# State-space layers: the transfers of the chunk states are issued from ScalarE's queue instead of SyncE's

## The reference

```
for i in range(4):
    z = layernorm_channels(h, ln_w[i], ln_b[i])
    dtA = (-exp(A_re_log) + 1j * A_im) * exp(log_dt)
    C = (C_re + 1j * C_im) * expm1(dtA) / A
    K = 2 * Re(sum_n C * exp(dtA * l))          # l = 0 .. L-1
    y = gelu(causal_convolution(z, K) + z * D_skip)
    out = W @ y + b
    h = out[:H] * sigmoid(out[H:]) + h
```

## Time and profile before

| | us |
|---|---|
| median of 3 runs | 1290.07 (1289.85 to 1290.78) |
| profiled execution, its own time | 1292.57 |
| its span | 1290.80 |
| PE busy | 1026.0 (79%) |
| DVE busy | 774.5 (60%) |
| ACT busy | 529.7 (41%) |
| POOL busy | 418.0 (32%) |
| states' matmuls (725) start in the four layers at | 115.37, 200.67, 286.68, 368.17 |

### The profile page before, as it was taken

One profiled execution on the slowest core, in us unless ns is written; L12 is line 12 of the kernel. 1 busy time (PEld: TensorE's weight loads), 2 busy tenths in 40 slices (PEclk: granted clock), 3 DMA queues, 4 the chain that ended last, 5 costly groups with the idle time before them and its releaser, 6 DMA issues.

```text
span 1290.8 us, 20116 instructions
## 1 busy us (share of the span) xinstructions
PE 1026.0 (79%) x7980; PEld 692.3 (54%) x7980; DVE 774.5 (60%) x1349; ACT 529.7 (41%) x1231; POOL 418.0 (32%) x488
## 2 busy tenths in 40 slices
PE   6895876858545189999999777769889789979887
PEld 3563654636423167878787652334456534546643
DVE  2574574654827534646464668969756557956644
ACT  4646555356123311222212060026686514767732
POOL 0724403324106500000000125439843434954420
PEclk9976967669666589999999988979899899979989
DMA  3307135063144374334631210000111210012101
GB/s 94 73 7 143 32 62 109 6 100 71 23 78 197 66 139 98 98 97 75 120 68 29 92 66 1 0 1 0 34 35 39 58 65 26 1 34 51 43 9 33
DMA packets 60479, 76.50 MB, mean 59 GB/s; under 512 B 37500, under 2 KB 41992, under 8 KB 58632
## 3 DMA queue, kind: packets, MB, share of 16 engines
q1 hardware_dynamic: 60396, 75.36, 25.8%
HBM read 52.87 MB, written 1.51 MB: 42 GB/s over the span
## 4 chain that ended last, share of the span: by engine, by line
PE 51%; DVE 16%; POOL 14%; ACT 5%; SPq 5%; DMA 4%; issue 4%; POOLq 0%; DVEq 0%
PE psum L1189 7%; PE psum L1191 6%; PE psum L1190 6%; POOL rest L1426 3%; POOL rest L1416 3%; POOL rest L1422 2%; PE psum L693 2%; PE psum L1670 2%; SPq L1012 2%; POOL rest L1452 2%; DVE main L506 2%; SPq L1018 2%; PE psum L1716 2%; PE psum L1663 2%; DMA rest<-share_d 2%
## 5 line engine op out<-in xcount | busy, mean ns | idle before, releaser
L406 POOL TENSOR_TENSOR kept<-kept 128x8 f32<-128x8 f32 x8 | 1.6, 202 | 401.5 <-DVE kept L383 401.5
L1375 ACT ACTIVATE rest<-psum,main 128x128 f32<-128x128 f32 x256 | 113.3, 482 | 11.6 <-POOL main L1437 8.9
L1036 ACT ACTIVATE x_high<-main 128x512 fp32r<-128x512 f32 x48 | 30.3, 633 | 199.4 <-DVE main L1110 199.4
L1189 PE MATMUL psum<-x_high,w_low 128*128 128x512 f32 x192 | 76.9, 400 | 20.1 <-DVE x_low L1115 20.1
L1452 POOL TENSOR_TENSOR rest<-rest,main 128x512 f32<-128x512 f32 x64 | 65.4, 1042 | 34.6 <-DVE main L1522 34.6
L1189 PE MATMUL psum<-hid_high,w_low 128*128 128x512 f32 x192 | 75.6, 394 | 0.7 <-DVE main L1134 0.7
L1190 PE MATMUL psum<-x_low,w_high 128*128 128x512 f32 x192 | 76.2, 397 | 0.0
L1191 PE MATMUL psum<-x_high,w_high 128*128 128x512 f32 x192 | 76.1, 396 | 0.0
L1190 PE MATMUL psum<-hid_low,w_high 128*128 128x512 f32 x192 | 74.8, 389 | 0.0
L1191 PE MATMUL psum<-hid_high,w_high 128*128 128x512 f32 x192 | 74.7, 389 | 0.0
L1110 DVE TENSOR_TENSOR main<-kept,rest 128x512 f32<-128x512 f32 x48 | 33.1, 690 | 68.1 <-PE psum L1191 43.8
(11 more groups left out here) (316 smaller groups left out, 2841.2 us busy)
## 6 DMA issues: line engine op xcount, KB each, us to landing
rest<-share_d SPq DMA_DIRECT2D x4, 3072.0 KB, 21.4
rest<-share_d SPq DMA_DIRECT2D x4, 2304.0 KB, 20.4
main<-main SPq DMA_DIRECT2D x32, 256.0 KB, 5.2
main<-k_pad SPq DMA_DIRECT2D x16, 512.0 KB, 7.5
rest<-main SPq DMA_DIRECT2D x32, 256.0 KB, 3.5
main<-w_dram SPq DMA_DIRECT2D x2, 3072.0 KB, 14.0
main<-rest SPq DMA_DIRECT2D x32, 128.0 KB, 4.4
rest<-tables_dram SPq DMA_DIRECT2D x2, 2048.0 KB, 8.7
```

The source lines that it names most:

```text
L1189: T.matmul(dst, w_small, x_large, start=first, stop=False)
L1375: last = A.activation(probs[:, p, 4 * r + m, :], bank[2 * p + r][:, m * P:(m + 1) * P], ACT.Exp, scale=row_scale[:, c, r, m:m + 1], bias=r ...
```

## The change

In SP's part of a layer the loop of eight transfers is taken out. In ACT's part the same eight, with the same waits on `s4_u` and the same increments of `s4_u_moved`, stand behind the near sines and ahead of the far sines. In the last layer, where there are no sines, they stand behind the copies of `K`. ACT's wait for `s4_u` ahead of the gelu is dropped, as the transfers have waited for the same value.

```
@@ s4_act_layer
             if more:
                 s4_act_sines_near(act, L + 1)
+            for ri, src in ((0, u_re), (1, u_im)):
+                act.wait_ge(sem("s4_u"), L * 2 + ri + 1)
+                for g in range(GROUPS):
+                    at = CHUNK + MODES * ri
+                    act.dma_start(zu[at:at + MODES, HG * g:HG * (g + 1), :], src[32 * g:32 * g + 32]).then_inc(sem("s4_u_moved"), 16)
+            if more:
                 s4_act_sines_far(act, L + 1)
                 s4_act_magnitudes(act, L + 1, LOW_BANKS)
             A.activation(warm[:, 3 * L + 2:3 * L + 3], warm[:, 0:1], ACT.Gelu_apprx_tanh)
-            act.wait_ge(sem("s4_u"), L * 2 + 2)
@@ s4_sp_layer
-            for ri, src in ((0, u_re), (1, u_im)):
-                sp.wait_ge(sem("s4_u"), L * 2 + ri + 1)
-                for g in range(GROUPS):
-                    at = CHUNK + MODES * ri
-                    sp.dma_start(zu[at:at + MODES, HG * g:HG * (g + 1), :], src[32 * g:32 * g + 32]).then_inc(sem("s4_u_moved"), 16)
```

## The result

The changed kernel runs in 1284.78 us (median of 20 runs), the one before in 1290.12 (20 runs). The ratio is 0.9967, with a 95% interval of 0.9954 to 0.9980: 4.3 us less, between 2.6 and 5.9 (this is how far the means of the runs lie apart; the medians differ by 5.3). In a later comparison of the same two it was 0.9953 (0.9937 to 0.9968). The forecast was 1280.8, 9.3 us less. The direction was right, the size twice what was measured.

A forecast was written before the change was run, and what follows sets the result against it. Bound: Toeplitz reads, then states, filling the DMAs without pause ahead of PE. Gains of 2.3, 2.3 to 2.4, 2.3 and 2.3 us in layers 0 to 3 sum to 9.3, from 1290.07 to 1280.8; range 1276.5 to 1291.

The forecast's parts named there:

- What bounds the kernel: Ahead of PE's line 725: Toeplitz reads, then states, fill the DMAs without pause; PE idles 62.4 us in four layers.
- The landing: States' arrival ahead of PE: both streams mixed at 296 GB/s, 92 more than one, gain 2.3 us a layer.
- The hand-over: Quarter microsecond where Toeplitz reads give way to states on SP's queue: 288 and 304 GB/s, taken as the mixed rate.
- The full overlap: Rival at the states' landing: Toeplitz data alone end it, 4.5 us sooner; 12.9 us in all, 1277.2; chance 0.20.
- one stream at a time: Rival in the DMA engines: large and small packets taken in turn, 0.8 us a layer, 3.3 in all, 1286.8; chance 0.22.
- the estimate of 3.6 us: Sum over four layers if two halves at once give 6% of 15 us, by the Trainium skill.
- Held up: Rival at ACT's issues: stuck behind SP's backlog, ACT free at 111.53 in layer 0; 6 us slower, 1296; chance 0.16.
- What ACT pays: Ahead of the far sines: four u_im issues at 0.64, 2.56 us; ACT delayed 5.3, hidden under its wait for PE.
- The powers and POOL's norm: Work on DVE and POOL moving with ACT: powers to about 119.1 under the gelu; norm has some 8 us slack.
- Behind it every step shifts alike: After the last gelu of each layer: later steps move by the same gain, 2.3 us in layer 3.

The follow-up runs named there:

- (3): Changed kernel with the eight state transfers left out in layers 1 to 3; 1277.64 us, ratio 0.9891 to the kernel before (four runs).
- (1): Changed kernel with its state transfers cut into runs of 256 bytes by reversed row order; 1285.90 us, ratio 0.9966 to the kernel before.
- 2: Kernel before, one queue, with the four u_re transfers ahead of the fourth Toeplitz read; 1286.99 us, ratio 0.9979.
- 6: Kernel before, one queue, with the fourth Toeplitz read behind all eight state transfers; 1291.65 us, ratio 1.0004.
- 7: Changed kernel with the eight state transfers issued by GpSimd instead of ACT; 1285.15 us, ratio 0.9970 to the kernel before.
- 9: Changed kernel with each Toeplitz read spread over 128 partitions instead of 64 in layers 1 to 3; 1281.81 us, one run.
- (8): The changed kernel once more, unaltered, as a measure for other runs; 1283.65 us, ratio 0.9953 to the kernel before.
- (10): Kernel before, one queue, with the state transfers' bytes spread over all 128 partitions in layers 1 to 3; 1283.33 us, one run.
- (4): Changed kernel with only u_re issued by ACT, u_im by SP behind the Toeplitz reads; 1289.13 us, ratio 0.9994 to the kernel before.
- (5): Changed kernel with the state transfers' bytes spread over all 128 partitions in layers 1 to 3; 1278.82 us, one run.

## Why the prediction was off

**What bounds the kernel: right, and half heeded.** That the queue never pauses, and that 3.15 MB fill the time to the landing, was read from the earlier trace rows and holds. (3) shows it by taking the states' 1.05 MB out.

**The landing: the term that was mis-sized.** The step is "I take 2.3, as it is the only rate measured with both kinds in flight". The hand-over's quarter microseconds at 288 and 304 were taken for the rate of two streams running side by side. The stretch with two queues moves 230 and 233: 26 to 29 more than 204, for 8.7 us (the states' packets in layer 0 run from 6.1 to 14.9 us) instead of 5.1, so 26 x 8.7 / 204 = 1.1 us. The starts moved by 1.2 to 1.7; the rest, up to 0.6 us, is not accounted for.

The hand-over's rate wasn't even a rate. Its quarter microsecond in layer 0, before:

```profile
DMA packets 127, 0.07 MB, mean 288 GB/s; under 512 B 116, under 2 KB 116, under 8 KB 127
q1 hardware_dynamic: 127, 0.07, 157.1%
```

The view counts a packet's bytes in full where it starts (by its size classes 11 packets of 4 KB and 116 of 256 bytes or less). These eleven are 45 of the 72 KB, and one takes about 1.035 x 16 / 50 = 0.33 us (an estimate from the earlier trace rows), longer than the window. The packets that start in the window take 157% of the engines' time in it. With each packet's bytes spread over its own time, the trace gives 211 GB/s here and 207 in layer 1, hardly more than one stream's 203; over six microseconds around the hand-over the view itself shows no more than 212:

```profile
106.00:112.00 6.00, 0.00 (x0) 0.00 (x0) 3.00 (x4) 4.34 (x4) 0.76 (x2) 0.50 1.23 212
```

So no row of before measured two streams at once, and the 92 GB/s that the term was made of weren't there. The prediction had another objection among the words on its rival ("it may be different engines on different streams") and gave it too little weight; this trace can't tell whether that is so.

**The full overlap was out of reach.** Its argument, less than half of the rate of 455 for each stream, holds for the states (340 when spread) and not for the Toeplitz rows (218 when spread). That both move the same alone, 203 and 202, was read as one cause for both, and it is two. The overlap's own ceiling was a little low besides: 4.5 us, where the Toeplitz data alone in (3) gave 5.1 to 5.6.

**The rival "one stream at a time" came nearest**, with 0.8 us a layer and 1286.8, but by luck: its mechanism in the form given, by turns between a large and a small packet, would have left the Toeplitz data 1/16 of the bytes, and they had half. The Trainium skill (DMA: Bandwidth & Descriptors, Issuing engines are not separate DMA queues) says that DMAs of several issuing engines interleave on the same 16 and that only issue time is saved. The trace agrees with the first (0.91 and 0.93 MB side by side in 8 us) and not wholly with the second: the pair moves 13% more than one stream (230 against 203), and 7% more in (1) (217). The 6% of SBUF — State Buffer, "Can I just issue two DMAs to hit both halves?", is the right order of size, and the estimate of 3.6 us made from it was closer to 4.3 than my 9.3.

**"Held up" was wrong.** ACT's issues take 0.51 to 0.68 us, the one of 0.68 at 100.86, while SP stood 3.19 us in its fourth Toeplitz issue from 100.67 on. What is full is SP's queue, and ACT's is another.

**What ACT pays: right.** The cost of 0.64 for each issue was 0.54 to 0.66 (four in 105.52 - 103.02 = 2.50 us), `u_im`'s wait decided, as said, and the four of `u_re` cost nothing, for they begin at 99.59 while line 777 is still running. Far sine to warm-up took 8.86 us (105.52 to 114.38) where 8.85 was forecast. The far sine starts 105.52 - 103.00 = 2.52 us behind `u_im`, against 2.56. The powers and POOL's norm caused no wait.

**Behind it every step shifts alike: not in layer 3.** There the start gained 1.5 us and the transpose 0.6. The matmuls took 6.19 us instead of 5.30. TensorE's granted clock in the first 4 us of them, after and before:

```profile
361.46:365.50 4.04, 4.04 (x153) 4.04 (x157) 0.00 (x0) 1.39 (x2) 0.00 (x0) 0.50 0.02 4
```

```profile
368.17:372.20 4.03, 4.03 (x180) 4.03 (x184) 0.00 (x0) 1.52 (x2) 0.00 (x0) 0.60 0.02 4
```

Ahead of them PE was idle for 21.1 us (22.6 before the change). From the first matmul on the clock now stays at 0.50 (1.2 GHz) for 5.1 us, longer than the stretch shown; before, it went to full (2.4 GHz) after 3.2 us, within the stretch. So 153 matmuls are done there instead of 180. The other kernels show the same order in layer 3: started at 17.6, 17.6, 17.4 (before, 2, 6) the matmuls take 5.30, 5.41, 5.56 us, at 16.9 (1, 7, 9) 5.66, 5.70, 5.88, at 16.3 (8) 6.10, at 15.7 (10) 6.39 and at 12.5 (3) 6.38; (4), at 18.1, has 5.37, and (5), at 16.6, 5.71. In layers 0 to 2 the changed kernel's durations are those of before within 0.2. So in the last layer an earlier start went with longer matmuls, by up to 1 us; that the start is the cause isn't shown, as no run changed the clock alone.

## What to carry to other kernels

A transfer that is issued too late is worth moving only if the DMA engines have room at the earlier time: multiply bytes by the rate of each stream and see whether they fill the stretch, before counting the issue time as a gain. Two streams with the same rate can have different limits, so leave one out, or spread it over all partitions, to see which; a second queue overlaps them only as far as neither fills the engines by itself. And a rate over a stretch that is shorter than its packets is no rate: read it over many packets' time, queue by queue.

## What the runs showed of the hardware

- ACT's sequencer issues DMAs while its engine computes: the first at 99.59, with an activation from 98.38 to 100.29.
- Rows of 256 bytes from DRAM move at 240 GB/s in the first 1.5 us and at 203 from then on the earlier trace rows, and 290 in this part of it; why they slow down stays open. The kernel before, layer 0:

```profile
99.50:100.20 0.70, 0.70 (x2) 0.33 (x1) 0.67 (x2) 0.67 (x2) 0.00 (x0) 0.50 1.28 290
```

- Two queues with unlike packets share the DMA engines by bytes rather than by packets here: 0.91 MB in 3572 packets beside 0.93 MB in 352 in the same 8 us of layer 0.
- GpSimd issued four transfers of 128 KB in 2.22 us, 0.56 each, no slower than ACT or SP:

```profile
100.90 2.22 POOL L984 DMA_DIRECT2D main<-rest  x4 [27.40 <-DVE rest L566]
```
